# Token importance by exponential and reciprocal, constant products for three batches, and a new table of hop positions in an audio tower on one core

## The reference

```python
z = gelu(gelu(f @ mlp_w1 + mlp_b1) @ mlp_w2 + mlp_b2)       # f: 128 tokens x 128 channels, after four convolutions
imp = sigmoid((z @ mlp_w3 + mlp_b3)[..., 0]) + 1e-5         # importance of a token, one number for each
imp = imp / sum(imp) * (T / 2)
cs = cumsum(imp)                                            # ramps of cs weigh the tokens: 128 become 64
h = relu(norm(pooled))                                      # out of the tokenizer: (32, 128, 64)
h = h + attention(layernorm(h))                             # a delta rule over 128 steps, as a triangular solve
h = h + product_key_memory(layernorm(h))                    # 8 heads, 16 of 4096 keys and values for each row
```

## Time and profile before

| what | value |
|---|---|
| time, median of 3 runs | 3488.09 us (3485.33 to 3497.85) |
| profiled execution, its own time | 3483.99 us |
| its span | 3482.2 us, so 1.8 us lie around it |
| TensorE, VectorE, ScalarE, GpSimd busy | 89%, 82%, 63%, 71% of the span |
| granted TensorE clock, mean | 0.966 of full |
| first and last gather start | 171.6 and 3444.7 us |
| 80 gathers of one batch | 101.0 to 102.3 us from batch 4 to batch 28 |

### The profile page before, as it was taken

How to read it: one execution, slowest core, us unless ns; L and a number is a source line. 1 busy time by engine, 2 the same in 40 slices (tenths; PEclk the granted TensorE clock), 3 DMA queues, 4 the chain that set the end, 5 groups by cost and what they waited for, 6 DMA issues and landing times.

```text
span 3482.2 us, 78652 instructions
## 1 busy us (share of the span) xinstructions
PE 3109.2 (89%) x25496; PEld 2383.5 (68%) x25496; DVE 2848.4 (82%) x14914; ACT 2196.0 (63%) x5983; POOL 2469.7 (71%) x2571
## 2 busy tenths in 40 slices
PE   8779989999999999999989999999999999899778
PEld 6446767667676766767676676767767776666666
DVE  2568898888889888888988888888888889888763
ACT  3546666666666766666676666676667667666433
POOL 0076777777777777777777777777777777777774
PEclk9869999999999999999999999999999999999888
DMA  7022222222222222222222222222222222222222
GB/s 157 2 64 63 64 74 73 75 69 75 66 68 75 74 75 69 75 67 67 74 74 75 68 75 65 69 74 74 74 68 75 64 71 74 74 75 67 69 61 54
DMA packets 307371, 245.80 MB, mean 71 GB/s; under 512 B 246600, under 2 KB 259440, under 8 KB 306832
## 3 DMA queue, kind: packets, MB, share of 16 engines
q0 software_dynamic: 81920, 167.94, 18.3%
q1 hardware_dynamic: 225040, 72.83, 8.9%
HBM read 230.06 MB, written 10.49 MB: 69 GB/s over the span
## 4 chain that ended last, share of the span: by engine, by line
PE 51%; DVE 24%; ACT 18%; issue 5%; POOL 2%; DMA 1%; SPq 0%; DVEq 0%; ACTq 0%; POOLq 0%
PE bank L1374 13%; PE bank L1173 8%; DVE d_w L2216 4%; ACT L1447 3%; PE bank L1194 3%; PE bank L1159 3%; PE bank L1354 2%; PE bank L1352 2%; DVE dist L2168 2%; ACT d_w L1659 2%; PE bank L1156 2%; POOL got L1084 2%; DVE topi L1971 1%; PE bank L1268 1%; PE bank L1430 1%
## 5 line engine op out<-in xcount | busy, mean ns | idle before, releaser
L1084 POOL DMA_INDIRECT got<-in_table,rows x2560 | 2466.7, 964 | 975.1 <-issue 765.7
L1374 PE MATMUL bank<-d_w,tab 128*128 128x128 f32 x6144 | 1071.8, 299 | 100.9 <-DVE d_w L2216 89.7
L1374 PEld LDWEIGHTS bank<-d_w,tab 128*128 128x128 f32 x6144 | 839.2, 197 | 298.7 <-DVE d_w L2216 210.8
L2216 DVE SCALAR_TENSOR_TENSOR d_w<-bank,d_w 128x256 f32<-128x256 f32 x1536 | 625.6, 415 | 222.6 <-ACT d_w L1659 217.4
L1659 ACT ACTIVATE d_w<-bank 128x256 f32<-128x256 f32 x1536 | 580.9, 382 | 268.0 <-PE bank L1354 252.8
L1352 PE MATMUL bank<-stacked,stack_sel 128*128 128x128 bf16 x3072 | 430.6, 223 | 1.5 <-issue 1.5
L1354 PE MATMUL bank<-d_dist,sel 128*128 128x128 bf16 x3072 | 430.0, 223 | 0.0
L1173 PE MATMUL bank<-h,conv_w 128*128 128x512 f32 (+2 forms) x1024 | 333.1, 473 | 3.6 <-DVE h L1795 2.3
L1352 PEld LDWEIGHTS bank<-stacked,stack_sel 128*128 128x128 bf16 x3072 | 310.5, 103 | 22.1 <-issue 2.5
L2168 DVE TENSOR_REDUCE dist<-pick 128x32 f32<-128x512 f16 x384 | 261.8, 682 | 6.6
L1173 PEld LDWEIGHTS bank<-h,conv_w 128*128 128x128 f32 x1024 | 175.3, 193 | 124.5 <-issue 111.9
(11 more groups left out here) (328 smaller groups left out, 6372.7 us busy)
## 6 DMA issues: line engine op xcount, KB each, us to landing
got<-in_table,rows POOLq DMA_INDIRECT x2560, 2.5
stacked<-parts SPq DMA_DIRECT2D x576, 64.0 KB
parts<-d_parts SPq DMA_DIRECT2D x32, 288.0 KB, 2.2
stacked<-parts SPq DMA_DIRECT2D x576, 16.0 KB
tab<-in_table SPq DMA_DIRECT2D x24, 256.0 KB, 7.3
got<-in_pairs SPq DMA_DIRECT2D x1, 2048.0 KB, 9.2
shared<-in_x SPq DMA_DIRECT2D x32, 50.0 KB
mlp<-in_mw SPq DMA_DIRECT2D x1, 1024.0 KB, 9.0
```

Source lines behind the costliest of these rows:

```text
L1084: pool.indirect_dma_start(got[:, n % NGB, k, :], None, table, bass.IndirectOffsetOnAxis(ap=rows[:, b % 2, g * TOPK + k:g * TOPK + k + 1], ...
L1374: last = mm(acc_bank[:, i * P:(i + 1) * P], tab[:, i, 2 * tile + x, :], d_w[:, u % 2, x, :], start=tile == x == 0, stop=tile == TILES - 1 ...
L2216: stt(both, pair_bank[u % 2][:, 2 * P:4 * P], TOPK - 0.5, both, ALU.is_lt, ALU.mult).then_inc(s_d_w, 1)
```

## The change

Three things change.

1. **The importance.** The sigmoid is computed as 1 / (1 + exp(-x)). In `imp_t` ScalarE issues one Exp with scale -1 and the bias `-b3`, with the table of Exp and Ln loaded after `z2` (now in batch 0 too) and no load of its own and none after it. In `imp` VectorE issues three instructions in place of one: plus one (with a ceiling of 1e38), a reciprocal, plus 1e-5, each 128 x 1, each waiting for the one before.
2. **The constant products.** `FILL` is keyed by batch and hop. It holds 380 products: 158 in batch 0, 183 in batch 1, 39 in batch 2. Of the 158 and 183, 193 stand ahead of the hop `simcp` of batch 0's mixer; before, all 212 did. On their way from there to the first `dt` (stage 4, batch 0) TensorE's hops have 166 more, then 21 in the hops `z1p` and `z2p` of batch 2.
3. **The positions.** All of `AT` and `OWN` are new. The entries of `OWN` for batches 1, 2, 29, 30 and 31 now repeat `AT` but for a few numbers; before, almost each of their numbers was its own. Batch 0's tokenizer keeps its own. Some positions (in steps, for a batch in the middle):

| hop | before | after |
|---|---|---|
| `rows` of route | 1.999 | 2.046 |
| `a0` | 2.494 | 2.601 |
| `a4` | 3.044 | 3.162 |
| `dt` | 2.427 | 2.472 |
| dense units ordered behind `a4` in batch 31 | 20 | 23 |

On TensorE `a0` of batch 0 stands ahead of `z1p` and `z2p` of batch 2 before, and behind them after.

```diff
-FILL = {"start": 4, "c1": 9, "c2": 9, "c3": 9, "v0": 3, "v1": 3, "v2": 3, "v3": 3, "k1": 14, "w1": 3, "k2": 13, "w2": 2, "k3": 10, "w3": 1,
-        "z1p": 8, "z2p": 10, "cums": 18, "pool": 5, "w4": 1,
-        "xd": 11, "proj": 1, "lora": 6, "ss": 9, "tri": 16, "p0": 12, "p1": 2, "p2": 2, "p3": 2, "p4": 2, "t0": 1, "t1": 1, "t2": 1, "t3": 1, "t4": 1, "og_t": 6, "x2": 6, "sims": 4}
+FILL = {(0, "start"): 4, (0, "c2"): 6, (0, "v2"): 3, (0, "v3"): 3, (0, "k1"): 22, (0, "w1"): 3, (0, "k2"): 14, (0, "w2"): 3, (0, "k3"): 10, (0, "w3"): 2, (0,
+        "z2p"): 6, (0, "cums"): 15, (0, "pool"): 6, (0, "w4"): 2, (1, "c0"): 4, (1, "v0"): 3, (0, "proj"): 6, (0, "lora"): 5, (0, "ss"): 10,
...
+        (1, "offsol"): 1, (1, "sol2"): 2, (1, "o"): 2, (2, "w2"): 2, (1, "x2"): 7, (1, "sims"): 4, (2, "z1p"): 15, (2, "z2p"): 6}
...
         AT = (
             (
-                -198748, -111759, -111385, -100343, -54192, -50171, -16364, 27459, 53455, 114376, 114377,
...
+                -150469, -126999, -125820, -85999, -85521, -29163, -16733, 9167, 107578, 137177, 158128,
...
-            def filled(hop):
+            def filled(b, hop):
-                for _ in range(FILL.get(hop, 0)):
+                for _ in range(FILL.get((b, hop), 0)):
                     mm(acc_bank[:, 0:P], const("ident"), const("ones"), start=True, stop=True)
...
                 act.wait_ge(s_z2b, b + 1)
                 a(z2[:, :], z2[:, :], ACT.Gelu).then_inc(s_z2, 1)
-                if b > 0:
-                    exp_and_ln()
+                exp_and_ln()
...
-                a(imp[:, 0:1], z3[:, :], ACT.Tanh, scale=0.5, bias=half_b3[:, :]).then_inc(s_imp_t, 1)
-                exp_and_ln()
+                a(imp[:, 0:1], z3[:, :], ACT.Exp, scale=-1.0, bias=minus_b3[:, :]).then_inc(s_imp_t, 1)
...
-                ts(half_b3[:, :], mlpb[:, MC:], 0.5, None, ALU.mult)
+                ts(minus_b3[:, :], mlpb[:, MC:], -1.0, None, ALU.mult)
...
                 vec.wait_ge(s_imp_t, b + 1)
-                ts(imp[:, 1:2], imp[:, 0:1], 0.5, 0.5 + 1e-5, ALU.mult, ALU.add).then_inc(s_imp, 1)
+                ts(imp[:, 0:1], imp[:, 0:1], 1.0, 1e38, ALU.add, ALU.min).then_inc(s_imp_sum, 1)
+                vec.wait_ge(s_imp_sum, b + 1)
+                v.reciprocal(imp[:, 0:1], imp[:, 0:1]).then_inc(s_imp_inv, 1)
+                vec.wait_ge(s_imp_inv, b + 1)
+                ts(imp[:, 1:2], imp[:, 0:1], 1e-5, None, ALU.add).then_inc(s_imp, 1)
```

More of the change, by code:

```diff
@@ L165, in tower @@
         mlpb2 = sb("mlpb2", [P, MLP])
-        half_b3 = sb("half_b3", [P, 1])
+        minus_b3 = sb("minus_b3", [P, 1])
         proj = sb("proj", [P, NSTACK])
@@ L337, in tower @@
         s_z2b, s_z3, s_imp_t, s_imp = sem("s_z2b"), sem("s_z3"), sem("s_imp_t"), sem("s_imp")
+        s_imp_sum, s_imp_inv = sem("s_imp_sum"), sem("s_imp_inv")
         s_cums = sem("s_cums")
@@ L493, in tower @@
             (
[6 rows of a table removed]
-            (
[6 rows of a table removed]
-            (
[3 rows of a table removed]
-            (
[5 rows of a table removed]
-            (
[21 rows of a table removed]
-            (
-                2200281, 2493586, 2506386, 2516835, 2549163, 2574473, 2688447, 2733115, 2733116, 2747597,
-                2748528, 2840571, 2863130, 2878843, 2887791, 2891381, 2924672, 2925927, 2927609, 2937285,
-                3009655, 3044347, 3082042, 3086571, 3119830,),
-            (
[9 rows of a table removed]
[6 rows of a table added]
+            (
[6 rows of a table added]
+            (
[3 rows of a table added]
+            (
[5 rows of a table added]
+            (
[21 rows of a table added]
+            (
+                2182451, 2601196, 2601197, 2611263, 2612117, 2612118, 2804229, 2805947, 2807697, 2812657,
+                2845578, 2874368, 2880867, 2884559, 2892960, 2897093, 2939554, 2950200, 2951118, 2961095,
+                2961104, 3162419, 3181512, 3181594, 3237119,),
+            (
[9 rows of a table added]
         )
@@ L1098, in _ @@
             mm(mx[:, 0:4], const("center"), chan[:, 0:4], start=True, stop=True).then_inc(s_bias_ps, 1)
-            def filled(hop):
-                for _ in range(FILL.get(hop, 0)):
+            def filled(b, hop):
+                for _ in range(FILL.get((b, hop), 0)):
                     mm(acc_bank[:, 0:P], const("ident"), const("ones"), start=True, stop=True)
-            filled("start")
+            filled(0, "start")
             pe.wait_ge(s_conv0_ready, 1)
@@ L1137, in first_conv @@
                         yield f"c{r}"
-                        filled(f"c{r}")
+                        filled(0, f"c{r}")
                         pe.wait_ge(s_norm0, r - 1)
@@ L1141, in first_conv @@
                     yield f"v{r}"
-                    filled(f"v{r}")
+                    filled(0, f"v{r}")
                     squares(r)
@@ L1150, in tokenizer @@
                     yield f"c{r}"
+                    filled(b, f"c{r}")
                     if r == 0:
@@ L1157, in tokenizer @@
                     yield f"v{r}"
+                    filled(b, f"v{r}")
                     pe.wait_ge(s_sq0, b * 4 + r + 1)
@@ L1161, in tokenizer @@
                     yield f"k{n}"
-                    if b == 0:
-                        filled(f"k{n}")
+                    filled(b, f"k{n}")
                     pe.wait_ge(s_pad, b * 3 + n)
@@ L1175, in tokenizer @@
                     yield f"w{n}"
-                    if b == 0:
-                        filled(f"w{n}")
+                    filled(b, f"w{n}")
                     variance(b, n - 1)
                 yield "z1p"
-                if b == 0:
-                    filled("z1p")
+                filled(b, "z1p")
                 if isinstance(b, int) and b == 0:
@@ L1189, in tokenizer @@
                 yield "z2p"
-                if b == 0:
-                    filled("z2p")
+                filled(b, "z2p")
                 pe.wait_ge(s_z1, b + 1)
@@ L1198, in tokenizer @@
                 yield "cums"
-                if b == 0:
-                    filled("cums")
+                filled(b, "cums")
                 pe.wait_ge(s_feat, b + 1)
@@ L1206, in tokenizer @@
                 yield "pool"
-                if b == 0:
-                    filled("pool")
+                filled(b, "pool")
                 pe.wait_ge(s_ramp, b * 6 + 6)
@@ L1211, in tokenizer @@
                 yield "w4"
-                if b == 0:
-                    filled("w4")
+                filled(b, "w4")
                 variance(b, 3)
@@ L1220, in mixer @@
                 yield "xd"
-                if b == 0:
-                    filled("xd")
+                filled(b, "xd")
                 dve("ln")
@@ L1229, in mixer @@
                 yield "proj"
-                if b == 0:
-                    filled("proj")
+                filled(b, "proj")
                 act("xd")
@@ L1240, in mixer @@
                 yield "lora"
-                if b == 0:
-                    filled("lora")
+                filled(b, "lora")
                 dve("sig_g")
@@ L1247, in mixer @@
                 yield "ss"
-                if b == 0:
-                    filled("ss")
+                filled(b, "ss")
                 dve("kks")
@@ L1253, in mixer @@
                 yield "tri"
-                if b == 0:
-                    filled("tri")
+                filled(b, "tri")
                 dve("rk2")
@@ L1264, in mixer @@
                     yield f"p{lv}"
-                    if b == 0:
-                        filled(f"p{lv}")
+                    filled(b, f"p{lv}")
                     dve("bonus" if lv == 0 else f"t{lv - 1}")
@@ L1269, in mixer @@
                     yield f"t{lv}"
-                    if b == 0:
-                        filled(f"t{lv}")
+                    filled(b, f"t{lv}")
                     act(f"p{lv}")
@@ L1276, in mixer @@
                 yield "rhs0"
-                if b == 0:
-                    filled("rhs0")
+                filled(b, "rhs0")
                 dve("t4")
@@ L1281, in mixer @@
                 yield "sol1"
-                if b == 0:
-                    filled("sol1")
+                filled(b, "sol1")
                 act("rhs0")
@@ L1286, in mixer @@
                 yield "offsol"
-                if b == 0:
-                    filled("offsol")
+                filled(b, "offsol")
                 act("sol1")
@@ L1291, in mixer @@
                 yield "sol2"
-                if b == 0:
-                    filled("sol2")
+                filled(b, "sol2")
                 act("offsol")
@@ L1296, in mixer @@
                 yield "o"
-                if b == 0:
-                    filled("o")
+                filled(b, "o")
                 dve("sa")
@@ L1302, in mixer @@
                 yield "og_t"
-                if b == 0:
-                    filled("og_t")
+                filled(b, "og_t")
                 dve("og")
@@ L1307, in mixer @@
                 yield "wo"
-                if b == 0:
```

(8 more changed lines are left out.)

## The result

The changed kernel takes 3447.75 us (median of 4 runs, 3444.27 to 3452.39), the kernel before beside it 3486.71 us (3481.09 to 3497.85). The ratio is 0.9883, with a 95% interval of 0.9859 to 0.9907. That is 39 us less; 20 had been forecast against the median of the runs shown (16 against the profiled execution).

What follows compares the result with a forecast made beforehand. GpSimd's 2560 gathers, 1.269 us each, were taken to bound the kernel. From 3484.0 us: first gather -6.0, early waits -7.6, middle -5.0, late waits -1.4, tail +4.0, giving 3468 us; range 3446 to 3493, the forecast's own 3455 to 3480.

Steps and rivals of the forecast that it cites:

- first gather: Start of the execution: GpSimd's first gather would start 6 us earlier, at 165.6 us.
- early waits: Three waits of GpSimd in the first batches, 12.6 us beyond usual gaps: 7.6 us of them would go.
- middle: From 352 to 3137 us, GpSimd's waits lose 7.4 us: the new positions would win back 5.
- tail: Behind the last gather: three more dense units would cost 4.0 us, bounds 0 and 10.
- I take 4.0: Ahead of batch 0's first `simcp`: nineteen fewer constant products save 4.0 us, bounds a gain of 10 and a loss of 4.
- 2.0 for VectorE's run: VectorE's hops from 134.8 to 171.6 us, making batch 0's row numbers: shorter stalls gain 2.0 us, bounds 0 and 2.9.
- I count nothing for the period: Each batch: removing ScalarE's two loads gains nothing because the gathers cover them; 62 us if that cover is gone.
- The path over ScalarE: Rival: ScalarE's path, with its loads, binds every batch, so removing them gives 3420 us; chance 0.07.
- Given back: Rival: the start gains little and the tail loses up to 10 us, giving 3484 us; chance 0.26.
- The products stay at half clock: Rival: 166 products cost 74 us against 33 us idle at the start, giving 3508 us; chance 0.03.
- The new order starves the gathers: Rival: late `a0` or row numbers make GpSimd wait in every batch; at 2 us each, 3524 us; chance 0.07.
- the other engines keep nearly the same pace: In the middle batches, speeding ScalarE or TensorE could win back only GpSimd's 7.4 us of waiting.

Runs made afterwards that it cites:

- e1: The kernel before with the new importance alone, old products and old positions: 0.9984 of the kernel before.
- e14: The changed kernel with the old importance (Tanh and its loads), new products and positions kept: 1.0146 of the kernel before.
- e13: The kernel before with the new counts of constant products alone, old importance and positions: 0.9965 of the kernel before.
- e4: The kernel before with the new positions alone, old importance and products: 1.0248 of the kernel before.
- e5: The changed kernel without the 222 constant products of batches 1 and 2, batch 0's 158 kept: 0.9943 of the kernel before.
- e3: The changed kernel with the old positions, new importance and products kept: 0.9972 of the kernel before.
- e6: The changed kernel with no constant products at all: 1.0007 of the kernel before.
- e8: The changed kernel with 15 of the 16 row transfers of each group: 0.9814 of the kernel before, a batch of 101.26 us.
- e16: The changed kernel with 14 of the 16 row transfers of each group: 0.9798 of the kernel before, a batch of 101.34 us.
- e9: The kernel before with 15 of the 16 row transfers of each group: 0.9941 of the kernel before, a batch of 100.77 us.
- e10: The changed kernel with the old positions and 15 of 16 row transfers a group: 0.9901 of the kernel before.

## Why the prediction was right and wrong

The sign was right, and so was the mechanism in the middle. The size was half of what came: 3468 us forecast, 3447.75 measured, near the lower edge of the range. By the terms of the sum:

| term | forecast | measured |
|---|---|---|
| first gather | -6.0 | -17.8 |
| early waits | -7.6 | -12.6 |
| middle | -5.0 | -6.5 |
| late waits | -1.4 | +0.3 |
| scattered waits, gathers' own time | 0 | -2.0 |
| tail | +4.0 | -1.1 |
| sum | -16.0 | -39.7 |

**The step that failed is "I take 4.0" for the constant products ahead of the first gather**, which with 2.0 for VectorE's run made "the first gather starts 6 us earlier". The 2.0 is near in size: the last stretch shrank by 1.6 (by 2.1 in e1). It was right in part by luck: the stall of 1.7 fell to 0.4 as foreseen, but that on `z2p` stayed at 1.1 at full clock, and e14, with the old importance, has a last stretch of 35.7 against 35.2, so the importance is worth only 0.5 there. The 4.0 was 16.2, beyond even its bound of 10. It priced nineteen products fewer at 0.223 us and held that nothing else moved there. The clock of 0.81 from 65.5 to 83.5 us was never asked for, and the positions of batches 0 and 1 were not costed at the start at all. e13, e4 and e14 show that the products were a gain of 3 alone and that it took both parts for 17.7. "I count nothing for the period" from the importance held for the old positions (e1).

**Early waits.** The 5 us kept back for `a0` of batch 0 behind `z1p` and `z2p` of batch 2 did not come: e5 brings a wait of 10.2 us there back without the later products, so these paid for themselves. The wait of 7.15 us for batch 1's row numbers goes with the positions: e3, with the old ones, still has its whole 6.85 above a usual gap; e5 and e6 have none.

**The rivals.** *The path over ScalarE* is out: the importance alone gave -0.16%, and even with 15 transfers a batch stayed the same. *Given back* is out. *The products stay at half clock* is out: the clock is 1.00 until 200 us, and 0.97 from 118 to 250, the stretch in which all of the 187 products behind `simcp` run. *The new order starves the gathers* is the one that mattered: its condition is just what e4 and e14 show, at a price of 3.1 to 3.4 us a batch in place of its 2, at the place it named (the first group's row numbers). The new importance is what averts it. So it was wrong to cost the positions and the importance apart: with the old positions the importance is worth nothing (e13 and e3) to 6 us (e1), with the new ones 2.6% or some 92 us (e14 and all: 1.0146 and 0.9883).

**"GpSimd has no free time" and "the other engines keep nearly the same pace"** were both right, and the second was understated. A batch of 101.4 us is a near tie of two loops, which no reading of GpSimd's own rows could tell.

**The tail.** Three more dense units were charged 4.0 us; the tail shrank by 1.1. TensorE in order of time, against the earlier trace rows:

```profile
3403.22 1.99 PE L1381 MATMUL bank<-got,spread_w 128*32 128x128 f32 x24
...
3408.62 1.06 PE L1381 MATMUL bank<-got,spread_w 128*32 128x128 f32 x8 [3.40 <-DMA got<-in_table,rows]
...
3435.55 1.44 PE L1359 MATMUL bank<-d_w,tab 128*128 128x128 f32 x8 [0.21 <-DVE d_w L2203]
```

Before, TensorE came to the last group at 3447.22, just as its last rows landed (3444.7 and 2.5), and had all 32 halves of the sum to do. Now it has done 24 of them ahead of time and waits 3.40 us for the last rows. The sum ends 2.6 us behind the last gather in place of 4.4 (-1.8). The 23 units then take 27.3 us, until 3436.99, where twenty took 26.4 (+0.9): the three more cost 0.9 in all, where the prediction gave each the 1.32 of the others. Behind the last unit lie 5.5 us in place of 5.7 (-0.2). Why a unit takes 1.19 us now and 1.32 before is not told apart: no run moved the tail alone.

Of the signs that the prediction named, the period of 101.4 us and the gap of 0.3 us in the middle came. The first gather came ahead of its 160 to 172 us, the tail of 35.5 below its 38 to 44, and GpSimd's waits beyond the usual gaps were 6.3 us in place of some 13.

## What to carry to other kernels

Where several parts of a change meet on one in-order queue, cost each with the others in place too: here positions alone lost 2.5% and the whole won 1.2%. Read the granted clock of every stretch of the start, not only the last before the first result, and price filler work by the clock it keeps as well as by its time. An engine that is shown never to wait can still have another loop 0.2% to 0.9% behind it (new and old order here); cutting its work in an experiment is a quick way to see that before a faster version of it is written.

## What the runs showed of the hardware

The mean time of the same gather is not fixed: 963 ns in the changed kernel, 955 and 956 in e4 and e14, 956 and 953 in e8 and e16. In 2560 gathers 8 ns are 21 us. GpSimd waits more in these four than in the changed kernel, but it does so in e9 and e10 too, where the mean is 969 and 970; so what sets it stays open. TensorE's clock was granted at 0.81 in a stretch in which its records are busy for 15.88 of 18.00 us, and at 1.00 in one with 11.59 of 12.10. A product that does nothing thus shortened the chain that it stood in: 380 of them, 0.223 us each on the chain, are 85 us of TensorE's time, and the kernel with none is 1.2% slower than the one with all.
